# A decoder layer on one core: expert batches of 40 and 24 rows instead of 48 and 16, a new spacing of the shared and read-back groups, and no work for a round behind the last

## What is computed

```python
x = layernorm(x + linear_attention(x))            # 16 heads of 8, softplus features, cumulative sums
x = layernorm(x + cross_attention(ctx, x))        # 16 heads of 64, keys from the context and x
x = layernorm(x + moe(x))                         # 8 experts, top 2, width 176, plus a shared MLP of width 352

logits = x @ gate_w.T;  scores = softmax(logits);  topk_w, topk_i = top_k(scores, 2)
topk_w = topk_w / (topk_w.sum(-1, keepdims=True) + 1e-20) * 2.5
y[t] = sum over the two experts e of token t:  topk_w * (silu(x[t] @ w_gate[e]) * (x[t] @ w_up[e])) @ w_down[e]
out = layernorm(x + y + (silu(x @ sw_gate) * (x @ sw_up)) @ sw_down)
```

## Time and profile before

| | before |
|---|---|
| median of 3 runs | 2062.98 us (2062.4 to 2067.14) |
| the profiled execution | 2065.15 us |
| its span, first to last instruction | 2063.4 us |
| PE, DVE, ACT, POOL busy | 95%, 73%, 62%, 63% of the span |
| granted TensorE clock, mean | 0.978 |

### The profile page before, as it was taken

The page is one execution under the profiler, slowest core; times in us unless marked ns, Lnnn a source line. Parts: engine busy times, 40 slices in busy tenths (PEclk is TensorE's granted clock), DMA queues, the critical chain, the costliest instruction groups (busy, mean ns, idle before and its releaser), DMA issues. The chain is left out here.

```text
span 2063.4 us, 47458 instructions
## 1 busy us (share of the span) xinstructions
PE 1966.8 (95%) x16023; PEld 1704.1 (83%) x16023; DVE 1508.9 (73%) x3953; ACT 1278.5 (62%) x3908; POOL 1307.8 (63%) x1462
## 2 busy tenths in 40 slices
PE   7999879999999999999999999999999989999976
PEld 4555469999999999999999999998899878788855
DVE  5999946777777777777777777778777755455575
ACT  4777646666666666666666666666666644444455
POOL 5888746666666666666666666666666664344476
PEclk9999979999999999999999999999999989999987
DMA  4200000000000000000000000001000022222354
GB/s 133 73 18 19 18 26 1 17 17 16 16 14 22 17 16 16 17 19 17 15 16 20 16 17 17 14 21 31 20 16 16 14 62 71 84 70 70 95 158 134
DMA packets 105023, 75.78 MB, mean 37 GB/s; under 512 B 11045, under 2 KB 98677, under 8 KB 104661
## 3 DMA queue, kind: packets, MB, share of 16 engines
q1 hardware_dynamic: 93732, 53.66, 9.3%
q0 software_dynamic: 8640, 17.97, 2.6%
q10 hardware_dynamic: 2416, 1.12, 0.2%
HBM read 40.15 MB, written 32.57 MB: 35 GB/s over the span
## 5 line engine op out<-in xcount | busy, mean ns | idle before, releaser
L1036 POOL TENSOR_TENSOR x_prob<-x_prob,x_inv 128x496 f32<-128x496 f32 x514 | 521.6, 1015 | 460.4 <-DVE x_inv L1186 457.7
L1114 ACT ACTIVATE x_prob<-x_ps_S,x_nmax 128x248 f32<-128x248 f32 x1028 | 472.7, 467 | 226.1 <-DVE x_nmax L1180 224.4
L1180 DVE TENSOR_REDUCE x_nmax<-x_ps_S 128x2 f32<-128x496 f32 x515 | 344.8, 670 | 105.0 <-PE x_ps_S L858 97.0
L1128 ACT COPY x_probT<-x_ps_T 124x512 f32<-124x512 f32 x512 | 300.2, 586 | 166.4 <-PE x_ps_T L1368 163.8
L856 PE MATMUL x_ps_S<-x_kT_lo,x_G_hi 128*128 128x248 f32 x1030 | 328.6, 319 | 0.0
L1368 PE MATMUL x_ps_T<-ident,x_prob 128*124 128x128 f32 x2048 | 319.0, 278 | 7.7 <-POOL x_prob L1036 6.4
L1368 PEld LDWEIGHTS x_ps_T<-ident,x_prob 128*124 128x124 f32 x2048 | 233.2, 140 | 73.9 <-POOL x_prob L1036 29.9
L858 PE MATMUL x_ps_S<-x_kT_hi,x_G_hi 128*128 128x248 f32 x1030 | 285.9, 278 | 0.0
L857 PE MATMUL x_ps_S<-x_kT_hi,x_G_lo 128*128 128x248 f32 x1030 | 285.7, 277 | 0.0
L1606 POOL DMA_INDIRECT sorted_results<-e_y,w_wkv x142 | 148.8, 1048 | 169.6 <-DVE e_y L1730 160.7
L1338 PE MATMUL x_ps_O<-x_probT,x_V 124*64 124x128 f32 x4096 | 251.9, 276 | 0.4 <-ACT x_probT L1128 0.4
(11 more groups left out here) (246 smaller groups left out, 4474.7 us busy)
## 6 DMA issues: line engine op xcount, KB each, us to landing
w_wkv<-sorted_rows SPq DMA_DIRECT2D x142, 66.0 KB
e_back<-sorted_results SPq DMA_DIRECT2D x28, 256.0 KB, 3.6
x_nk<-latents SPq DMA_DIRECT2D x34, 124.0 KB
latents<-lin_nlat SPq DMA_DIRECT2D x32, 128.0 KB, 1.8
turned_rows<-w_rows SPq DMA_DIRECT2D x32, 128.0 KB, 1.7
w_wq<-turned_rows SPq DMA_DIRECT2D x32, 128.0 KB, 2.3
out_dram<-e_result SPq DMA_DIRECT2D x16, 256.0 KB, 3.6
x_nk<-in_ctx SPq DMA_DIRECT2D x34, 120.0 KB, 2.3
```

What stands on the lines that cost most here:

```text
L1036: nc.gpsimd.tensor_tensor(prob[:, k], prob[:, k], inv[:, k].unsqueeze(2).broadcast_to([P, 2, K]), ALU.mult).then_inc(prob_ready, 1)
L1114: nc.scalar.activation(prob[:, k, h, :], ps_S[:, n % BANKS, h * K:(h + 1) * K], ACT.Exp, bias=nmax[:, k, h:h + 1], accum_out=total[:, k, h ...
L1128: nc.scalar.copy(probT[0:KT, s % (2 * GANG)], ps_T[0:KT, s % 2, :]).then_inc(probT_ready, 1)
L1180: nc.vector.tensor_reduce(nmax[:, k, :], ps_S[:, n % BANKS, 0:2 * K].rearrange("p (h k) -> p h k", h=2), AX, ALU.max, negate=True).then_in ...
```

## The change

The kernel's lines move down by up to 19. Three things are edited.

First, the batches: 40 and 24 rows, so 87 and 55 blocks, still 142 in all, and 10 groups (`WHOLE`) of the first batch instead of 12. Second, cross attention leaves out all that round 31 made for a round 32 (and the context work for rounds 32 and 33). Third, the expert stage has a new timetable: shared groups start nine steps apart (`EVERY`), so that each has two steps without a piece; the read-back of the 10 first groups starts at steps 99, 103 and so on to 135 (before 115 to 142), that of the six others at 152 to 162 (before four at 152 to 158); within a group the delays are other, and `e_vare` and a new `e_minus` are made by ACT (`spread`), `e_shift` by POOL behind the root. SP issues all loads of the last groups, and its stores come five steps earlier in its stream.

```diff
-PER = (48, 16)
+PER = (40, 24)
...
-                    weights(unit + s + 2, (s + 2) % RINGS)
+                    if unit + s + 2 < ROUNDS * UNITS:
+                        weights(unit + s + 2, (s + 2) % RINGS)
...
-                    scores((unit + s + LEAD) % BANKS, (s + LEAD) % 2, par if ahead < PAIRS else 1 - par, ahead % 2)
-
-                    if u == 0:
-                        ahead = j + 3
+                    if r < FINAL or ahead < PAIRS:
+                        if u:
+                            pe.wait_ge(G_lo_ready, r * PAIRS + ahead + 1)
+                        scores((unit + s + LEAD) % BANKS, (s + LEAD) % 2, par if ahead < PAIRS else 1 - par, ahead % 2)
+
+                    ahead = j + 3
+                    if u == 0 and (r < FINAL or ahead < PAIRS):
...
-                    if s == 4:
+                    if s == 4 and r < FINAL:
...
-                    if u:
+                    if u and (r < FINAL or j < 4):
...
-    BACKS = 5
+    BACKS = 6
...
+    EVERY = 9
...
-    BACK_TIME = [FIRST_BLOCK[1] + AHEAD + 5 * g // 2 if g < WHOLE else TOTAL + 10 + 2 * (g - WHOLE) for g in range(GROUPS)]
+    BACK_TIME = [FIRST_BLOCK[1] + AHEAD + 4 * g if g < WHOLE else TOTAL + 10 + 2 * (g - WHOLE) for g in range(GROUPS)]
...
-                g, k = divmod(t - SHARED_FROM, PIECES)
-                if g >= GROUPS - LATE:
+                g, k = divmod(t - SHARED_FROM, EVERY)
+                if g >= GROUPS - LATE or k >= PIECES:
...
-            starts = [SHARED_FROM + PIECES * g for g in range(GROUPS)]
+            starts = [SHARED_FROM + EVERY * g for g in range(GROUPS)]
...
-                    for g in (WHOLE, WHOLE + 1):
+                    for g in range(WHOLE, GROUPS):
...
-                g = back_at(t, 8, 7)
+                g = back_at(t, 3, 6)
                 if g is not None:
                     store(g)
...
-                wait(pool, shift_ready, g - DEEP + 1)
-                pool.wait_ge(vare_ready, g + 1)
+                wait(pool, result_ready, (g - DEEP + 1) * GROUP)
+                pool.wait_ge(vare_ready, (g + 1) * 2)
                 nc.gpsimd.tensor_tensor(rstd[:, g % DEEP], vare[:, g % DEEP], slots.half[:], ALU.pow).then_inc(rstd_ready, 1)
+                pool.wait_ge(rstd_ready, g + 1)
+                nc.gpsimd.tensor_tensor(shift[:, g % DEEP], minus[:, g % DEEP], rstd[:, g % DEEP], ALU.mult).then_inc(shift_ready, 1)
...
+            def spread(g):
+
+                act.wait_ge(mom_ready, (g + 1) * GROUP)
+                wait(act, shift_ready, g - DEEP + 1)
+                nc.scalar.activation(vare[:, g % DEEP], mom[:, g % DEEP, :, 1], ACT.Identity, bias=slots.eps[:], scale=1.0
+                                     ).then_inc(vare_ready, 1)
+                nc.scalar.activation(minus[:, g % DEEP], mom[:, g % DEEP, :, 0], ACT.Identity, scale=-1.0
+                                     ).then_inc(vare_ready, 1)
...
-                    g = back_at(t, 6 + pair, 5 + pair)
+                    g = back_at(t, 7 + pair, 4 + pair)
...
-                v.tensor_scalar(vare[:, g % DEEP], mom[:, g % DEEP, :, 1], EPS, None, ALU.add).then_inc(vare_ready, 1)
-
-            def shifts(g):
-
-                dve.wait_ge(rstd_ready, g + 1)
-                v.scalar_tensor_tensor(shift[:, g % DEEP, :], mom[:, g % DEEP, :, 0], -1.0, rstd[:, g % DEEP, :], ALU.mult, ALU.mult
-                                       ).then_inc(shift_ready, 1)
...
-                g = back_at(t, 1, 1)
+                g = back_at(t, 2, 1)
                 if g is not None:
                     add_back(g)
-                g = back_at(t, 2, 2)
+                g = back_at(t, 3, 2)
                 if g is not None:
                     moments(g)
```

More of the change, by code:

```diff
@@ L883, in cross_attention @@
     GANGS = UNITS // GANG
-    SETS = 6 + (BATCHES + 1) * EXPERTS
+    SETS = 7 + (BATCHES + 1) * EXPERTS
     MADE = FIRST[1] // 2 + 2
+    FINAL = ROUNDS - 1
     U32 = mybir.dt.uint32
@@ L1050, in body @@
                         slots.scatter(pool, r - 2, 0, s - 14)
-                    if s == 6:
+                    if s == 6 and r < FINAL:
                         keys_hi(r + 1, 1 - par)
-                    if s == 7:
+                    if s == 7 and r < FINAL:
                         keys_lo(r + 1, 1 - par)
@@ L1060, in body @@
                         slots.empty_rows(pool, slots.empty, 0, s // 2 if s < 6 else 2)
-                    if s == 11:
+                    if s == 11 and r + 1 < FINAL:
                         context_deviation(r + 2)
-                    if s in (12, 13):
+                    if s in (12, 13) and r + 1 < FINAL:
                         normalise_context(r + 2, par, s - 12)
@@ L1119, in body @@
                 for s in range(UNITS):
-                    exponentials(unit + s + 2, (s + 2) % RINGS)
+                    if unit + s + 2 < ROUNDS * UNITS:
+                        exponentials(unit + s + 2, (s + 2) % RINGS)
                     if s == 10 and r:
@@ L1128, in body @@
                     nc.scalar.copy(probT[0:KT, s % (2 * GANG)], ps_T[0:KT, s % 2, :]).then_inc(probT_ready, 1)
-                    if s % 2 == 0:
-                        ahead = s // 2 + 3
+                    ahead = s // 2 + 3
+                    if s % 2 == 0 and (r < FINAL or ahead < PAIRS):
                         G_hi(r * PAIRS + ahead, ahead % 2)
@@ L1206, in body @@
                         V_copy(r * 8 + 3, 0, 1, 1)
-                    if s and s % 2 == 0:
+                    if s and s % 2 == 0 and (r < FINAL or j < 5):
                         k = j - 1
                         V_copy(r * 8 + 4 + k, 1 - k // 4, k % 4 // 2, k % 2)
-                    if s == 5:
+                    if s == 5 and r < FINAL:
                         keys(r + 1)
-                    if s % 2:
+                    if s % 2 and (r < FINAL or j + 3 < PAIRS):
                         G_lo(r * PAIRS + j + 3, (j + 3) % 2)
@@ L1224, in body @@
                             slots.table(dve, 0, k)
-                    maxima(unit + s + LEAD, (s + LEAD) % RINGS)
-                    inverse(unit + s + 2, (s + 2) % RINGS)
-                    if s == 7:
+                    if unit + s + LEAD < ROUNDS * UNITS:
+                        maxima(unit + s + LEAD, (s + LEAD) % RINGS)
+                    if unit + s + 2 < ROUNDS * UNITS:
+                        inverse(unit + s + 2, (s + 2) % RINGS)
+                    if s == 7 and r + 1 < FINAL:
                         context_moments(r + 2, par)
@@ L1385, in body @@
                         output(r - 1)
-                    if s == 4:
+                    if s == 4 and r < FINAL:
                         pe.wait_ge(V_ready, r * 8 + 4 + 2)
                         keys(r + 1, 1 - par)
-                    if u:
+                    if u and (r < FINAL or j < 4):
                         if s == 3 and later_round(r):
                             pe.wait_ge(sum_ready, r)
-                        elif s == 5:
+                        elif s == 5 and r < FINAL:
                             pe.wait_ge(kT_ready, r + 2)
@@ L1628, in _ @@
                     scatter(i)
[L1629 removed]
+                g = back_at(t, 5, 3)
                 if g is not None:
@@ L1696, in _ @@
                     slots.scores_of(act, LAST)
+                g = back_at(t, 4, 3)
+                if g is not None:
+                    spread(g)
                 for pair in range(2):
-                    g = back_at(t, 6 + pair, 5 + pair)
+                    g = back_at(t, 7 + pair, 4 + pair)
                     if g is not None:
                         normalise(g, pair)
-                if t == TOTAL + 6:
-                    sent_after(act, TOTAL)
-                    for g in (WHOLE + 2, WHOLE + 3):
-                        for c in range(2):
-                            load_back(act, g, c)
         @block.vector
@@ L1770, in moments @@
                 dve.wait_ge(stat_ready, (g + 1) * GROUP)
+                wait(dve, vare_ready, (g - DEEP + 1) * 2)
                 for k in range(GROUP):
                     v.bn_aggr(mom[:, g % DEEP, k, :], stat[:, k, :]).then_inc(mom_ready, 1)
[L1773 to L1781 removed]
             for t in range(STEPS_ALL):
```

20 lines of the change are left out of this document (7 added, 13 removed).

## The result

The changed kernel takes 2052.82 us (median of 8 runs, 2049.23 to 2054.95), the kernel before 2062.69 beside it (8 runs, 2057.67 to 2068.11). The ratio is 0.9948, 95% interval 0.9933 to 0.9962: faster by half a per cent, some 10 us. The forecast was 2047 us, with a range of 2032 to 2060. The profiled execution took 2051.95 us.

What follows compares the result with a forecast made beforehand. PE bounds the shared stretch; in the block stretch beside the read-backs engines wait in turn at a clock of 0.82. Terms -4.5, -15.7 and +4.7 give -15.5 us: 2065.15 to 2049.6, less 2.2 for the median, 2047; range 2032 to 2060.

Steps and rivals of the forecast that it cites:

- -15.7: Expert stage, steps 8 to 144: 323.9 us forecast against 339.6, with shared groups, read-backs and the last bare steps summed.
- Last round: Last round of cross attention: dropping PE's unused products saves 4.5 us; ends 0 and 7.8, the chain having slack.
- the last round gives nothing: Rival, chance 0.02: the chain through ACT, POOL and DVE sets the round's end; 4.5 us more, 2051 or 2052.
- Ninth step: Shared groups in the expert stage: nine steps make a group 21.1 us for 18.98, the addition to X unhidden; ends 20.5, 21.8.
- Read-back: Steps 99 to 134: reading back groups 0 to 7 under shared groups costs 3.5 us in all; ends 0 and 21.
- Not hidden: Rival, chance 0.13: each read-back costs 2.6 us in the shared stretch too; 2064 us, no change.
- the clock falls: Rival, chance 0.05: PE idles where DVE's work piles up in the shared stretch and its clock drops; 2073 us, slower.
- Steps 134 to 144: End of the block stretch: ten bare steps at 1.48 us plus 3.2 for groups 8 and 9, 18 us; ends 15 and 25.
- The stall for late rows: Shared stretch: 7.0 us above thirteen calm groups, mostly PE's stop for late rows, left in the sum unchanged.
- Tail: Behind block 141: six groups read back for four, 2.79 us each further one, 5.6, less 0.9: +4.7; ends 0 and 8.
- The 0.9: Tail: 0.9 us won back because group 9 is long through when group 14's shared product starts.

Runs made afterwards that it cites:

- the surplus work: Changed kernel, but cross attention again makes everything for the rounds behind the last, as in the kernel before; 2059.15 us, ratio 0.9961 to the kernel before.
- partners: Changed kernel with region-closing writes spread and the addition to X a step later, 2044.64 us; the same with cross attention's work for later rounds put back, 2045.80 us.
- old batches: Changed kernel with batches of 48 and 16 rows again, twelve groups read back at the old spacing; 2057.46 us, ratio 0.9967 to the kernel before.
- the closes spread: Changed kernel with SP's nine writes closing the second batch's regions sent one every second step from step 30, not all there; 2051.50 us, ratio 0.9938.
- the kernel with eight steps: Changed kernel with shared groups eight steps apart again (EVERY = 8), the rest unchanged; 2056.25 us, ratio 0.9947 to the kernel before.
- addition later: Changed kernel with DVE's addition of a shared group to X one step later, in the ninth step alone; 2052.52 us, ratio 0.9925 to the kernel before.

## Why the prediction was right, and where it was not

**The number.** 2047 was forecast, 2052.8 measured: faster, within the range, with two thirds of the gain. By the trace the terms came out -4.8, -17.3 and +6.0 for -4.5, -15.7 and +4.7, together -16.1 for -15.5; the 2.7 us lost ahead of cross attention make it -13.4, against 13.2 between the two spans. Between the medians it is 10 us, since the profiled execution of before lay 2.5 above its median and that of after 0.9 below. That the number came out is in part luck: the first trace of after was the only one with the cut in which DVE's pause did not eat the first term, and on the second chip the same kernel gained 6.3 us, and took 2059.25, just inside the range.

**Last round: -4.5.** The size fits the one trace where PE's work set the time. As a statement on the kernel the step failed: "the chain has about half of its length as slack" did not count a stop of DVE of 4 us, which stands in no trace with the surplus work, nor the clock, which fell in most of the traces with the stop. Whether the surplus work had covered this stop or kept it from coming, no run shows. The rival "the last round gives nothing" had 0.02; on another chip its place was right and its cause another (1.2 us between partners).

**Ninth step: a group 21.1 us.** 20.85, the two steps in the order forecast, with PE waiting 0.48 us for `e_xT_lo`; the surplus of 0.65 us for the addition was right, as its removal shows (0.5 to 0.65). But the comparison that the step was meant to carry, fourteen steps moved out of a stretch where each cost 2.8 us, did not hold. In the changed kernel's form such bare steps (without a shared piece) cost 2.0 at full clock. The ninth step itself neither gained nor cost more than 1 or 2 us.

**Read-back: 3.5 us for eight groups.** Steps 99 to 134 took 87.8 us (blocks 95 to 131), 4.4 above four calm groups. No wait of `e_hsum` there, epsilon 295 ns on ACT. "Not hidden" and "the clock falls" did not happen. Of the 16.3 us that blocks 14 to 141 gained in the first trace, some 6 to 7 are the smaller first batch with its read-backs four steps apart (old batches, 6.6), and 10 the new delays, the nine steps and the move to ACT and POOL together. The ninth step gives nothing with the new batches, and the move 0.5 to 2.5, so most of the 10 falls to the new delays; but this is by elimination, since no run has the old delays in the changed kernel. The wait of `e_hsum` that was to go by the delays went only with the wider spacing.

**Steps 134 to 144: 18 us.** 18.9.

**The stall for late rows, left as it was.** It was mis-sized: blocks 32 to 50 took 48.1 us against 41.9 with the closes spread, so the stop costs 6.2; in the kernel before they took 47.6, against 43.0 in the kernel with eight steps that had almost no stop, so 4.6. I had seen that SP closes the regions at step 30 in both kernels and took that for no change. Why the kernel with eight steps kept only 0.63 us of the stop stays open: the kernel before has the same eight steps and the same step of the closes, and PE waited 2.51 us there.

**Tail: +4.7.** +6.0. The term of 2.79 us for a further group was mis-sized and is 3.09: POOL makes sum, root and product one behind the other (1.26, 1.48 and 0.20 us), and with the shift on DVE again it was 2.79 to 2.84. The 0.9 to be got back from group 9 is not to be seen.

**A reading of the rows.** The prediction says that DVE's epsilon is long where POOL is at work. In the trace of before it took 0.17 us at 1969.40 and 2030.94 too, beside POOL's root, and 1.74 to 1.85 only beside POOL's sum `e_back` and a scatter. Nothing in the sum hung on it.

## What to carry to other kernels

When engines wait for one another in turn, try first how far apart the items and the stages of one item stand: here that carried most of the gain (by elimination, as far as the stages are concerned), and the clock came back with it, while the spreading of the main work gave nothing. Removing work that nobody uses can bring out another engine's stop, so its removal should be judged on several executions and chips, not by a trace. A burst of transfers on the queue that also feeds the pipeline (here nine writes, 10 us) is worth 6 us when it is spread, and a wait that the profile puts down to a long finished engine can be the sign of it.

## What the runs showed of the hardware

- DVE stood still for 3.6 to 4.2 us at the same instruction, in most with no releaser in the profile, in ten of eleven traces with the cut and in none of the three without. Holding the row loads back did not change it. Its cause is open.
- PE's last product of 32 matmuls took 3.81 us at full clock, and 5.3 to 6.4 in traces in which PE had idled 2.0 to 3.6 us in front of it, part of it at half clock; in one of these (addition later) the clock had fallen 4.7 us before the product began. Twice it held the full clock after an idle time of 1.8 us.
- POOL's power of 128x4 took 1.01 us with DVE quiet (2044.46 in the trace of after), 1.04 beside four of DVE's statistics (2029.44) and also beside a sum `e_hsum` (1945.82), but 1.48 in the tail, where both a sum and the statistics behind it ran beside it. The Trainium skill (GPSIMD Engine Reference, Specifications) has GpSimd and VectorE share SBUF interfaces, with contention where a VectorE instruction has two SBUF inputs; the trace agrees only in part, since `e_hsum` has two and made no difference by itself (1.04).
- The same code ahead of cross attention reached it between 266.3 and 270.8 us. Differences of 4 us between single traces can be nothing but this.
